# Transposing DMAs in place of TensorE transposes between the products of a two-layer feed-forward pass

## The reference, cut to what matters

```python
# layer 1, feed-forward (F = 2048)
h2 = ln(x2) * g2 + beta2
x3 = x2 + gelu2(h2 @ W1 + b1) @ W2 + b2        # gelu2(x) = x * sigmoid(1.702 x)
# layer 2, one expert e per sequence (I = 2048)
y  = gelu(x3 @ Wi[e] + bi[e]) @ Wo[e] + bo[e]
r  = layernorm(x3 + y) * gamma[e] + beta[e]
# layer 3: first and second differences of r times grids, relu of r + dt * (their sum)
```

## Time and profile before

| | |
|---|---|
| median of 3 runs | 2524.64 us (2522.03 to 2525.68) |
| the profiled execution's own time | 2522.23 us |
| its span, first to last instruction | 2520.4 us |
| mean granted TensorE clock | 0.997 |
| TensorE, VectorE, ScalarE, GpSimd busy | 98%, 76%, 45%, 39% |
| DMA moved | 311.35 MB, mean 124 GB/s |

### The profile page before, as it was taken

The page is one execution under the profiler, slowest core; times in us unless marked ns, Lnnn a source line. Parts: engine busy times, 40 slices in busy tenths (PEclk is TensorE's granted clock), DMA queues, the critical chain, the costliest instruction groups (busy, mean ns, idle before and its releaser), DMA issues.

```text
span 2520.4 us, 45559 instructions
## 1 busy us (share of the span) xinstructions
PE 2471.3 (98%) x14444; PEld 1221.4 (48%) x14444; DVE 1904.1 (76%) x3666; ACT 1126.5 (45%) x2159; POOL 981.1 (39%) x840
## 2 busy tenths in 40 slices
PE   7999999999999999999999999999999999999997
PEld 5555555555555555544444444444444444444443
DVE  7878777777777685763588689678787886986777
ACT  3666767675758585742223223233222322232231
POOL 1464646464646464410044143242341440531331
PEclk9999999999999999999999999999999999999999
DMA  7444444544544445451232142133222322321341
GB/s 244 140 154 155 152 156 152 164 153 151 166 149 161 148 151 169 159 193 51 72 126 84 62 135 92 59 117 117 84 87 92 105 84 75 125 92 59 114 140 53
DMA packets 150228, 311.35 MB, mean 124 GB/s; under 512 B 16619, under 2 KB 21739, under 8 KB 150004
## 3 DMA queue, kind: packets, MB, share of 16 engines
q1 hardware_dynamic: 140788, 291.93, 35.4%
q10 hardware_dynamic: 9216, 16.78, 1.8%
HBM read 291.68 MB, written 16.81 MB: 122 GB/s over the span
## 4 chain that ended last, share of the span: by engine, by line
PE 52%; DVE 3%; issue 1%; ACT 0%; POOL 0%; DVEq 0%; ACTq 0%
PE bank L1522 17%; PE bank L1524 16%; PE bank L1523 16%; PE bank L1508 1%; PE bank L1598 1%; DVE g2T_hi L1857 1%; DVE g2T_lo L1858 1%; PE bank L1528 0%; DVE w_hi L1933 0%; ACT g L1690 0%; DVE stage L1820 0%; DVE stage L1801 0%; PE bank L1644 0%; PE bank L1632 0%; DVE w_lo L1933 0%
## 5 line engine op out<-in xcount | busy, mean ns | idle before, releaser
L1109 DVE CUSTOM_DVE_ANT_0 w_words<-bank,stage 128x512 f32<-128x512 f32 x512 | 323.8, 686 | 102.0 <-PE bank L702 93.7
L884 ACT ACTIVATE w_words<-w_words,nmax 128x512 f32<-128x512 f32 x512 | 363.6, 714 | 42.1 <-DVE nmax L1109 41.0
L564 POOL TENSOR_TENSOR stage<-stage,mask_add 128x1024 f32<-128x1024 f32 x128 | 273.1, 2144 | 230.1 <-DMA stage<-in_bias 213.2
L1857 DVE CAST g2T_hi<-g 128x512 f16<-128x512 f32 x256 | 178.8, 698 | 221.0 <-ACT g L1690 217.1
L725 PE MATMUL bank<-ident,w_words 128*128 128x128 f32 x2048 | 298.3, 280 | 11.6 <-DVE late L1124 5.9
L725 PEld LDWEIGHTS bank<-ident,w_words 128*128 128x128 f32 x2048 | 222.8, 140 | 170.8 <-issue 82.9
L1690 ACT ACTIVATE g<-bank,bi 128x512 f32<-128x512 f32 x128 | 88.0, 687 | 352.3 <-PE bank L1524 331.3
L1858 DVE TENSOR_TENSOR g2T_lo<-g,g2T_hi 128x512 f16<-128x512 f32 x256 | 238.7, 933 | 8.8
L1432 POOL TENSOR_TENSOR stage<-grid,f 128x512 f32<-128x512 f32 x84 | 141.3, 1708 | 195.5 <-DVE f L1760 74.0
L870 ACT ACTIVATE late<-bank 128x512 f32<-128x512 f32 x256 | 150.9, 590 | 147.4 <-PE bank L725 147.2
L1866 DVE SCALAR_TENSOR_TENSOR wl_lo<-stage,wl_hi 128x1024 f16<-128x1024 f32 x128 | 196.6, 1536 | 6.8 <-ACT wl_hi L1702 6.6
(11 more groups left out here) (299 smaller groups left out, 4894.8 us busy)
## 6 DMA issues: line engine op xcount, KB each, us to landing
stage<-in_bias SPq DMA_DIRECT2D x256, 512.0 KB, 4.4
stage<-in_W_l SPq DMA_DIRECT2D x128, 512.0 KB, 3.4
grid<-in_grids SPq DMA_DIRECT2D x140, 256.0 KB, 3.6
xin<-in_x SPq DMA_DIRECT2D x32, 256.0 KB, 4.1
x_rows<-w_words ACTq DMA_DIRECT2D x32, 256.0 KB, 3.7
out<-stage ACTq DMA_DIRECT2D x32, 256.0 KB, 2.0
late<-x_rows SPq DMA_DIRECT2D x7, 1024.0 KB, 8.3
l_rows<-in_rows SPq DMA_DIRECT2D x8, 768.0 KB, 6.2
```

The lines of the kernel that those rows point to most:

```text
L564: pool.tensor_tensor(bias[:, n % NB, :, :], bias[:, n % NB, :, :], mask_add[:, u % T, :].unsqueeze(1).to_broadcast([P, 2, S]), ALU.add).th ...
L884: act.activation(tile, tile, ACT.Exp, scale=-1.0, bias=nmax[:, u % 2, i:i + 1], accum_out=rsum[:, j, h:h + 1]).then_inc(prob_ready, 1)
L1109: dve.tensor_tensor_reduce(tiles[:, 4 * (u % NR) + i, :], bank[:, :], bias[:, half % NB, i % 2, :], -1.0, 3.0e38, ALU.add, ALU.min, nmax[: ...
L1857: link(dve.tensor_copy(gT[0][:, n % 4, :], g32[:, n % 2, :]))
```

## The change

1. Next norm. VectorE's h2 is no longer transposed on TensorE. In steps 26 and 27 ScalarE copies it, row tile by row tile, to a float16 hi tile, in steps 27 and 28 VectorE makes lo (both lie in the buffer `stage[:, 2:4]`, which is `prod`). When up 31 is done, SP issues 8 DMAs with transpose=True (4 tiles of hi, then 4 of lo, 128 x 512 float16 each) into `xT`. GpSimd's next alpha products wait for them.
2. x3. Tiles 0, 1 and 2 are split in SBUF by rows (`x3_halves`, in h2's buffer) and transposed by 6 DMAs of SP, in the order hi 0, hi 1, lo 0, lo 1, hi 2, lo 2, ahead of SP's loads of step 16. Tile 3 is still transposed on TensorE, by 4 transposes into bank 0.
3. The last four downs of the first half (12 to 15) come after up 15 and tile by tile: tile 0 and 1 with 12 to 14, then 15 for tile 0 and for tile 1, then tile 2 with all four, then tile 3. In the second half, too, no down stands between up 30 and up 31 now.
4. Ups 0 and 1 (from the second sequence on) and ups 16 and 17 are one group, `first_ups`: 16 matmuls with hi of `xT` for both, a wait for lo, then 4 with lo for the first and 4 for the second.

Semaphores are merged to make room for the new ones (splits_and_zeroed).

```diff
+                def transpose_x3():
+                    arrived(sp, it, ("up", NF - 1))
+                    sp.sem_inc(carrier, 1)
+                    for half, t in ((0, 0), (0, 1), (1, 0), (1, 1), (0, 2), (1, 2)):
+                        if half:
+                            sp.wait_ge(splits_and_zeroed, it * (2 * T) + t + 2)
+                        else:
+                            sp.wait_ge(hi_done, it * (2 * T) + t + 1)
+                        sp.sem_inc(carrier, 1)
+                        sp.dma_start(xT[half][:, :, t * P:(t + 1) * P], x3_halves[:, half, t, :], transpose=True)\
+                            .then_inc(transposed_in[half], 16)
...
-                loads = [(CHUNK[k - 2] if k >= 2 else -1, 0, load_chunk, (k,)) for k in range(NF)]
+                loads = [(NF, -1, transpose_x3, ())]
+                loads += [(CHUNK[k - 2] if k >= 2 else -1, 0, load_chunk, (k,)) for k in range(NF)]
...
+                if not is_last(it):
+                    arrived(sp, it, ("up", STEPS - 1))
+                    sp.sem_inc(carrier, 1)
+                    sp.wait_ge(splits_and_zeroed, it * (2 * T) + 2 * T + 1)
+                    sp.sem_inc(carrier, 1)
+                    for half in range(2):
+                        for t in range(T):
+                            sp.dma_start(xT[half][:, :, t * P:(t + 1) * P], h2_halves[half][:, t, :], transpose=True)\
+                                .then_inc(transposed_in[half], 16)
...
                 if not is_first(it):
+                    for half_in in transposed_in:
+                        pool.wait_ge(half_in, it * (2 * T - 1) * 16)
                     for t in range(T):
                         alpha_products(pool, it - 1, t)
...
+                def first_ups(half):
...
+                    pe.wait_ge(transposed_in[0], (it * (2 * T - 1) + half * (T - 1)) * 16)
+                    for n in range(2):
+                        for c in range(C):
+                            pe.matmul(first[n][:, :], ws[n][c][0], xT[0][:, c, :], start=c == 0, stop=False)
+                            pe.matmul(first[n][:, :], ws[n][c][1], xT[0][:, c, :], start=False, stop=False)
+                    pe.wait_ge(transposed_in[1], (it * (2 * T - 1) + half * (T - 1)) * 16)
+                    for n in range(2):
+                        for c in range(C):
+                            mm = pe.matmul(first[n][:, :], ws[n][c][0], xT[1][:, c, :], start=False, stop=c == C - 1)
+                        mm.then_inc(full_of(("up", half * NF + n)), 1)
...
+                def last_downs(half):
+                    lasts = range(NF - KEPT, NF - 1)
+                    for t, ks in ((0, lasts), (1, lasts), (0, (NF - 1,)), (1, (NF - 1,)), (2, (*lasts, NF - 1)), (3, (*lasts, NF - 1))):
+                        down_tile(half, t, ks)
...
                         run_stencil(0)
-                        for t in range(T):
-                            pe.wait_ge(x3_ready, it * T + T)
-                            for c in range(C):
-                                mm = pe.transpose(psum[c][:, t * P:(t + 1) * P], x2[:, t, c * P:(c + 1) * P], ident[:, :])
-                                if t == T - 1:
-                                    mm.then_inc(full_of(("x3T", c)), 1)
+                        pe.wait_ge(x3_ready, it * T + T)
+                        for c in range(C):
+                            mm = pe.transpose(psum[0][:, c * P:(c + 1) * P], x2[:, T - 1, c * P:(c + 1) * P], ident[:, :])
+                        mm.then_inc(full_of(("x3T", 0)), 1)
                         run_stencil(1)
                     for n in range(half * NF, half * NF + NF):
-                        up(n)
-                        if n - LAG_DOWN >= half * NF and not (is_last(it) and n - LAG_DOWN >= STEPS - KEPT):
+                        if n == NF or n == 0 and not is_first(it):
+                            first_ups(half)
+                        if n % NF > 1 or n < NF and is_first(it):
+                            up(n)
+                        if half * NF <= n - LAG_DOWN < half * NF + NF - KEPT:
                             down(n - LAG_DOWN)
...
-                    if half:
-                        pe.wait_ge(h2_ready, it * T + T)
-                        for c in range(C):
-                            h2_transposes(claim(pe, it, ("h2T", c)), c).then_inc(full_of(("h2T", c)), 1)
-                    for n in range(half * NF + NF - LAG_DOWN, half * NF + NF):
-                        down(n)
+                    if half == 0 or is_last(it):
+                        last_downs(half)
+                    else:
+                        for n in range(STEPS - KEPT, STEPS):
+                            down(n)
...
+                        x3_of(0)
+                        x3_of(1)
+                        x3_lo(0)
+                        x3_lo(1)
+                        x3_of(2)
+                        x3_lo(2)
+                        x3_of(3)
+                        dve.wait_ge(hi_done, it * (2 * T) + T)
+                        dve.tensor_tensor(xT[1][:, :, (T - 1) * P:], psum[0][:, :].rearrange("p (c q) -> p c q", c=C),
+                                          xT[0][:, :, (T - 1) * P:], ALU.subtract).then_inc(splits_and_zeroed, 1)
```

More of the change, by code:

```diff
@@ L1185, in ffn_pass @@
         if n == NF:
-            order += [(("x3T", c), c) for c in range(C)]
+            order.append((("x3T", 0), 0))
             in_ring(("L3", 0))
@@ L1217, in ffn_pass @@
         h2 = sb("h2", [P, T, D], F32)
+        x3_halves = h2[:, :, :].rearrange("p t d -> p (t d)").bitcast(F16).rearrange("p (h t d) -> p h t d", h=2, t=T)
+        h2_halves = [stage[:, 2 + i, :].bitcast(F16).rearrange("p (t d) -> p t d", t=T) for i in range(2)]
         f = sb("f", [P, T, D], F32)
@@ L1554, in up @@
                     mm.then_inc(full_of(("up", n)), 1)
+                def first_ups(half):
+                    ws = [[[x[:, n, c * P:(c + 1) * P] for x in wl] if half else [x[:, c, n * P:(n + 1) * P] for x in w1]
+                           for c in range(C)] for n in range(2)]
+                    first = [claim(pe, it, ("up", half * NF + n)) for n in range(2)]
+                    if half:
+                        pe.wait_ge(chunk_split, 1 + it * NF + 2)
+                        pe.wait_ge(splits_and_zeroed, 1 + it * (2 * T) + T)
+                    pe.wait_ge(transposed_in[0], (it * (2 * T - 1) + half * (T - 1)) * 16)
[8 more added lines that the diff above has]
+                        mm.then_inc(full_of(("up", half * NF + n)), 1)
                 def down(n):
@@ L1676, in sequence @@
                 prev = it - 1
-                def copy_hi(key, c):
-                    bank = arrived(act, it, key)
-                    act.activation(xT[0][:, c, :], bank[:, :], ACT.Copy).then_inc(hi_done, 1)
                 for n in range(STEPS):
                     if n == NF:
-                        for c in range(C):
-                            copy_hi(("x3T", c), c)
+                        for t in range(T - 1):
+                            act.wait_ge(x3_ready, it * T + t + 1)
+                            act.activation(x3_halves[:, 0, t, :], x2[:, t, :], ACT.Copy).then_inc(hi_done, 1)
+                        bank = arrived(act, it, ("x3T", 0))
+                        act.activation(xT[0][:, :, (T - 1) * P:], bank[:, :].rearrange("p (c q) -> p c q", c=C), ACT.Copy)\
+                            .then_inc(hi_done, 1)
                         act.wait_ge(rows_in, it * 32 + 32)
@@ L1707, in sequence @@
                         relu_store(act, prev, prev, SUM.index(n))
-                for c in range(0 if is_last(it) else C):
-                    copy_hi(("h2T", c), c)
+                    if n in (NORM2 + 3, NORM2 + 4) and not is_last(it):
+                        if n == NORM2 + 3:
+                            act.wait_ge(y_done, 1 + it * T)
+                            if is_first(it):
+                                act.wait_ge(w_split, len(PIECES))
+                        for t in range(2 * (n - NORM2 - 3), 2 * (n - NORM2 - 2)):
+                            act.wait_ge(h2_ready, it * T + t + 1)
+                            act.activation(h2_halves[0][:, t, :], h2[:, t, :], ACT.Copy).then_inc(hi_done, 1)
             sequence(0)
@@ L1983, in _ @@
                 if t >= 2:
-                    dve.wait_ge(full[t - 2], B + 1)
+                    dve.wait_ge(full[t - 2], (B if t == 2 else 0) + 1)
                     dve.wait_ge(out_ready, 1 + (B - 1) * T + t - 2)
```

72 lines of the change are left out of this document (31 added, 41 removed).

## The result

The changed kernel takes 2557.75 us in the median (2551.13 to 2563.49, 4 runs), the kernel before 2524.73 beside it: a ratio of 1.0132 (95% interval 1.0115 to 1.0148), 33 us more. The forecast was 2539 (14 us more): right in direction, less than half in size.

The account below looks back on a forecast made before the run. TensorE was taken as the bound, VectorE following closely. Seven sequences at +2.16 us (15.1) and the first at -0.9 gave +14.2: 2536.4 from the profiled 2522.23, median 2.4 above, say 2539 us; range 2520 to 2572.

Parts of the forecast that it names:

- norm off TensorE: At seven sequence ends, 16 TensorE transposes ahead of the next down go: -1.74 us each.
- down 2: Grouping ups 0 and 1 delays gelu 0; VectorE's chain to down 2 has no slack: +1.73 us a sequence.
- down 17: Grouping ups 16 and 17 delays gelu 16 and VectorE's chain to down 17: +1.73 us a sequence.
- down 15, tile 0: First half's last downs by tiles: down 15 waits for split 15, behind chunk 5's rest on VectorE: +1.4 us.
- middle and transposing DMAs: From the first stencil matmul to up 16: 0.96 us gained a sequence; the transposing DMAs cost 0.
- the first sequence: The sequence without a previous sequence's work on VectorE: -0.9 us in all.
- The transposing DMAs: 0: DMAs for x3 and the norm, 1.3 us apart on SP's queue, landing 1.7 after issue: nothing late, cost 0.
- slow transposes: Rival: transposing DMAs 2.0 us apart on SP's queue become the new wait, 33 us more, 2571 in all; chance 0.17.

Follow-up runs that it names:

- g1: Changed kernel plus some 120 filler waits on TensorE and some 20 on VectorE in the first sequence: 2539.32 us, ratio 1.0066.
- f2: e4's kernel plus some 70 filler waits on TensorE in the first sequence: 2511.19 us, ratio 0.9949 to the kernel before.
- h4: Kernel before with only the first half's last four downs tile by tile: 2533.72 us, ratio 1.0042.
- h1: Kernel before plus some 220 filler instructions on TensorE in the first sequence: 2530.27 us, ratio 1.0025.
- h2: Kernel before plus 7 filler instructions on VectorE in the first sequence: 2527.50 us, ratio 1.0017.
- f3: Changed kernel plus some 120 filler waits on TensorE alone in the first sequence: 2552.41 us, ratio 1.0118.
- f4: e1's kernel plus some 120 filler waits on TensorE in the first sequence: 2524.30 us, ratio 1.0008.
- e4: Kernel before with the norm transposed by early DMAs into h2's own buffer, old order of ups and downs: 2530.36 us, ratio 1.0034.
- e1: Changed kernel without the DMAs of lo halves, ups 0, 1, 16, 17 in the old order (result not the reference's): 2526.03 us, ratio 1.0009.
- e3: Kernel before with the norm's part alone: DMAs after up 31, last four downs behind it, ups 0 and 1 grouped: 2530.40 us, ratio 1.003.
- f1: Kernel before plus some 120 filler waits on TensorE in the first sequence: 2524.64 us, ratio 1.0006.
- e2: Changed kernel with down 12 of the first half back between ups 14 and 15: 2570.34 us, ratio 1.0202.

## Why the prediction was wrong

By its terms for one sequence, measured in g1, where no engine stops for code, against the kernel before; one pass stands for all, except for down 15. A gap is counted from one matmul's start to the next's, less 0.216.

| term | forecast | measured | from |
|---|---|---|---|
| norm off TensorE | -1.74 | -1.75 | passes of f2, 173.50 against 175.25 |
| down 2 | +1.73 | +1.60 | gap 1.78 against 0.18 |
| down 17 | +1.73 | +1.70 | gaps of down 16 0.12, up 19 0.46, down 17 1.66, less the 0.54 of before |
| down 15, tile 0 | +1.4 | +1.44 | mean of seven: none in sequence 1, 1.3 to 2.05 in the others; h4 alone 10.5 us / 7 = 1.5 |
| middle and transposing DMAs | -0.96 + 0 | -0.51 | 1516.64 to 1519.27 against 1511.51 to 1514.65 |
| sum | +2.16 | +2.48 | 7 times: 15.1 and 17.4 us; the first sequence -0.9 and -0.3; g1 is 17.8 over its kernel before |

- **The mechanism held.** The TensorE transposes were worth exactly what their row said, and VectorE's chains to downs 2, 17 and 15 gave it back. Up 19 I had not named: it waits for the bank that the later `total` frees, and takes part of down 17's lateness. The earlier trace rows I misread: its 2.9 us are those of the whole span, 0.4 a pass, which changes no term.
- **"The transposing DMAs: 0" was a little off.** The distance on SP was as assumed (issues of 1.20 to 1.27 us, 1.3 apart, except behind a late landing), the landing was not: 2.5 us, not 1.7. The rows of the issue in the changed kernel, lo and hi of x3, then the landing:

```profile
L1410 SPq DMA_TRANSPOSE hT_hi<-h x24: 1188/1197/1312, 1159.4 to 2420.2; - x24
L1410 SPq DMA_TRANSPOSE hT_lo<-h x24: 1188/1197/2172, 1162.1 to 2421.5; - x24
...
DMA to landing us min/median/max: 2.4/2.5/4.1
```

  That later landing is the 0.8 us for which the group waits in the middle in most passes (2.44 where a landing took 4.1). It halved the middle's gain, and in the first sequence the group waits 2.2 us. The halo DMAs that I took the landing from are in the same queue and the same memory but 40 times smaller. At the norm the group's hi products cover the lo halves wholly in g1 and but for up to 0.6 us in the changed kernel, whose lo halves are late by the fetched code.
- **The step that failed is the sum itself: it had no term for the code.** I took the passes as the same but for what the edit moves. The edit also made TensorE's code shorter and VectorE's longer, and both loops begin elsewhere. With the fillers the changed kernel takes 2539.3, the forecast's 2539 (17.8 over the kernel before beside it, where 14.2 was forecast); without them 18.4 us more. The profiled runs of the two, 14.5 us apart, show where: waits for splits 37.5 us against 29.4, waits for transposing DMAs 12.6 against 7.4, and some 1.5 us at half the clock behind a wait of 2.1 in one middle. The first comes from VectorE's stops and what is late behind them, the second from DMAs that land late beside fetched blocks. h1 and h2 show that the place stops an engine without any other part of the change. What a stop is worth depends on the slack behind it: f3 and f4 have nearly equal stops of VectorE (9.9 and 9.7 us), and down 0 waits 1.7 to 2.2 us in f3, which has the group, and at most 0.7 in f4, which hasn't. So place and change don't simply add.
- **Rival "slow transposes"** gave 2571, and the result lies between it and the forecast, but not by its mechanism, a distance of 2.0 us on SP: all waits for DMAs sum to 12.6 us, and the 5.2 by which they exceed g1's come with the fetched blocks. My range held the result, by luck: nothing in it stood for the code.

What stays open: why h1's stops are 0.7 to 1.2 us and e4's 2.1 to 2.6, when the filler was meant to put both at the same place of a block; why VectorE's stop is 1.1 us in h2 and 2 in f3; why it is missing in three of the changed kernel's restarts; and how a fetched block holds up a transposing DMA. The loaded blocks themselves are not seen, only their packets and the stops; that the block's edge is what stops the engine is inferred from how moving the code moves the stop.

## What to carry to other kernels

Read the packets of the instruction queues and the "issue" waits of both kernels before explaining a difference by data: in a loop that is fetched once at one place (98 packets) and at every restart at another (143), 7 idle instructions ahead of it on VectorE cost 0.2% (h2) and some 70 on TensorE gave back 0.8% (f2). The fetched code can cost by a stopped engine or by late DMAs, so compare the landing times of the two kernels too. When an operation is taken off the bounding engine, take it off without asking anyone else for anything earlier or later: e4's order, with its filler (f2), kept the whole 1.74 us per pass and is 0.5% faster than the kernel before, where the change as made lost 1.3%. A group of products that takes the lo half late finishes its first bank later, and a chain with no slack turns that into idle time nearly one for one (1.73 us of lateness, 1.60 and 1.70 of idle).

## What the runs showed of the hardware

- A transposing DMA of a 128 x 512 float16 tile inside SBUF takes 1.2 to 1.3 us of SP's queue and lands after 2.5 us; 104 of them raised the packets on q1 from 140788 to 197364. Where a block of code arrives between issue and landing, the landing takes up to 4.5 us and the next issue up to 2.2 (29 late of 104 in the changed kernel, none when filler alone keeps the code loaded: f3, g1).
- Returning to a loop's start can stop TensorE for 0.5 to 2.6 us (e1, e3, e4, h1) and VectorE for 1.1 to 2.6 us with no releaser; the same code, moved by idle instructions, doesn't stop. 46 fetched blocks more cost nothing measurable where no stop appears and no transposing DMA runs (f1).
- After a stop of 2.4 us between stretches of full work TensorE's granted clock was 0.50, its lower level of 1.2 GHz, for 3.4 us (e4, three of five restarts; e2 in six of eight middles, the one shown after a wait of 3.55). In the changed kernel it fell after a wait of 2.13 and stayed at 1.00 after one of 2.44; it stayed there after the stops of up to 2.5 in e3 and 1.8 in e1, so the length of the stop alone doesn't decide. So such a stop costs up to 1.7 us more than its wait shows: 8 matmuls at 0.43 in place of 0.216.
